# ScalarE writes the upper half of each gelu tile, VectorE only the lower half

## The reference, cut to what matters

```python
h = jax.nn.gelu(jnp.einsum('bsd,edh->bseh', x, w1) + b1, approximate=False)
expert_out = jnp.einsum('bseh,ehd->bsed', h, w2) + b2
out = jnp.einsum('bse,bsed->bsd', gates, expert_out)
```

## Time and profile before

| | |
|---|---|
| median of 3 runs | 2583.78 us (2581.89 to 2583.79) |
| the profiled execution | 2584.22 us |
| its span in the trace | 2582.4 us |
| second half in the trace | from about 1320 us to the end |
| busy over the span | PE 2400.6 us (93%), DVE 1714.1 (66%), ACT 1102.6 (43%), POOL 1118.8 (43%) |
| granted TensorE clock, mean | 0.969 |

### The profile page before, as it was taken

One profiled execution on the slowest core, in us unless ns is written; L12 is line 12 of the kernel. 1 busy time (PEld: TensorE's weight loads), 2 busy tenths in 40 slices (PEclk: granted clock), 3 DMA queues, 4 the chain that ended last, 5 costly groups with the idle time before them and its releaser, 6 DMA issues. The chain is left out here.

```text
span 2582.4 us, 36273 instructions
## 1 busy us (share of the span) xinstructions
PE 2400.6 (93%) x13556; PEld 1007.0 (39%) x13556; DVE 1714.1 (66%) x3957; ACT 1102.6 (43%) x2066; POOL 1118.8 (43%) x404
## 2 busy tenths in 40 slices
PE   7999799999999999999846899999999999999998
PEld 3444223333333232323223454544545454454543
DVE  4433587777777777777125567767676776767665
ACT  4332156666666666666612232323323242332320
POOL 0000369999999999999931112111011211102100
PEclk9999799999999999999968899999999999999999
DMA  7864402122130303130040001010100101010000
GB/s 245 291 226 159 111 11 70 50 52 70 32 91 14 87 25 80 31 104 18 18 156 30 17 1 63 1 53 11 46 17 1 62 1 60 4 46 17 1 17 17
DMA packets 130443, 155.00 MB, mean 60 GB/s; under 512 B 19838, under 2 KB 98174, under 8 KB 129245
## 3 DMA queue, kind: packets, MB, share of 16 engines
q1 hardware_dynamic: 130269, 152.69, 19.2%
HBM read 99.96 MB, written 52.17 MB: 59 GB/s over the span
## 5 line engine op out<-in xcount | busy, mean ns | idle before, releaser
L762 ACT ACTIVATE probs<-st_ps 128x512 f32<-128x512 f32 (+3 forms) x1280 | 610.3, 537 | 327.1 <-PE st_ps L865 179.7
L637 POOL TENSOR_TENSOR total<-total,probs 128x2048 f32<-128x2048 f32 (+3 forms) x200 | 706.5, 3532 | 47.6 <-ACT probs L762 26.6
L804 DVE TENSOR_REDUCE seg_max<-s_ps 128x1 f32<-128x512 f32 x768 | 506.1, 685 | 136.0 <-PE s_ps L851 133.8
L851 PE MATMUL s_ps<-k_pair,q_pair 96*128 96x512 f16 (+3 forms) x1280 | 435.0, 355 | 25.9 <-DMA q_pair<-q_parts 11.4
L865 PE MATMUL st_ps<-q_pair,k_pair 98*128 98x512 f16 (+3 forms) x1280 | 434.4, 353 | 25.7 <-ACT probs L762 16.5
L1429 PE MATMUL fps<-x2T,w_p_hi 128*128 128x512 f16 x1024 | 317.3, 379 | 0.0
L1429 PE MATMUL fps<-w_p_hi,hT 128*128 128x512 f16 x1024 | 306.0, 380 | 0.0
L885 PE MATMUL o_ps<-probs,v_sb 128*32 128x512 f32 (+3 forms) x2560 | 303.0, 546 | 0.0
L808 DVE CUSTOM_DVE_ANT_0 s_ps<-s_ps,later 128x384 f32<-128x384 f32 (+3 forms) x512 | 249.2, 500 | 66.2 <-issue 66.2
L1133 POOL TENSOR_TENSOR rstd<-rstd,keep_power 128x4 f32<-128x4 f32 x24 | 26.1, 1086 | 538.7 <-DVE rstd L1254 538.7
L865 PEld LDWEIGHTS st_ps<-q_pair,k_pair 98*128 98x128 f16 x1280 | 123.3, 98 | 328.1 <-ACT probs L762 233.5
(11 more groups left out here) (164 smaller groups left out, 3401.8 us busy)
## 6 DMA issues: line engine op xcount, KB each, us to landing
k_pair<-k_parts SPq DMA_DIRECT2D x96, 128.0 KB, 4.5
q_pair<-q_parts SPq DMA_DIRECT2D x96, 128.0 KB, 5.1
x_raw<-xT_in SPq DMA_DIRECT2D x8, 1024.0 KB, 6.2
q_parts<-qk_out SPq DMA_DIRECT2D x32, 256.0 KB, 4.1
k_parts<-qk_out SPq DMA_DIRECT2D x32, 256.0 KB, 4.1
piece_raw<-w_in SPq DMA_DIRECT2D x8, 1024.0 KB, 9.1
v_rows<-v_out SPq DMA_DIRECT2D x32, 256.0 KB, 2.1
w_parts<-piece_cut SPq DMA_DIRECT2D x8, 1024.0 KB, 6.0
```

What stands on the lines that cost most here:

```text
L637: last = nc.gpsimd.tensor_tensor(summed[:, :, off:], other[:, :, off:], probs[:, k % NP, :, off:], ALU.add)
L762: nc.scalar.activation(probs[:, k % NP, h, off:], st_ps[:, p % (2 * NVU) % RING, off:], ACT.Exp, scale=SCALE).then_inc(exp_done.sem, 1)
L804: nc.vector.reduce_max(highest, s_ps[:, slot], AX.X).then_inc(s_read.sem, 1)
L851: nc.tensor.matmul(s_ps[:, slot, 0:width], q_pair[a][0:NR, c, h, j * P:(j + 1) * P], k_pair[a][0:NR, h, s * CH:s * CH + width], start=True ...
```

## The change

ACT writes the upper half of each gelu tile itself, right behind the gelu, after waiting for its own gelu to be done. The wait that the upper half's buffer is free (`f_ready`, before the first of an expert's two tiles) moves with it, and the counter `h_hi` is now ACT's. DVE waits for the gelu and for `h_hi`, and writes the lower half as before. In a slot that is 16 instructions that leave DVE's queue and 16 that enter ACT's.

```diff
         @block.scalar
         def _(act):
-            lead(act, (act_read, hi_ready, exped, squared, gate_exped), (gelu_done,))
+            lead(act, (act_read, hi_ready, exped, squared, gate_exped), (gelu_done, h_hi))
...
                     act.wait_ge(h_lo.sem, at(h_lo, i, u, n - 2))
                     nc.scalar.activation(hidden[:, n % 2], fps[:, (u * NUNIT + f) % FB], ACT.Gelu,
                                          bias=W["b1_sb"][:, n:n + 1], scale=UN).then_inc(gelu_done.sem, 1)
+                    act.wait_ge(gelu_done.sem, at(gelu_done, i, u, n))
+                    if j == 0:
+
+                        act.wait_ge(f_ready.sem, at(f_ready, i, u, UNITS.index(("expert", e - 2, TT - 1)) if e >= 2
+                                                    else UNITS.index(("expert", E + e - 2, TT - 1)) - NUNIT))
+                    nc.scalar.activation(hT[:, 0, e % 2, j], hidden[:, n % 2], ACT.Copy,
+                                         scale=XS).then_inc(h_hi.sem, 1)
...
         @block.vector
         def _(dve):
             lead(dve, (dve_read, summed, spread, varied, normed, masked, smaxed, shifted, ssummed, inverted,
-                       square_held, routed), (h_hi, h_lo, added, summed3, spread3, varied3, normed3))
+                       square_held, routed), (h_lo, added, summed3, spread3, varied3, normed3))
...
                 if kind == "hidden":
                     n = 2 * e + j
                     dve.wait_ge(gelu_done.sem, at(gelu_done, i, u, n))
-                    if j == 0:
-
-                        dve.wait_ge(f_ready.sem, at(f_ready, i, u, UNITS.index(("expert", e - 2, TT - 1)) if e >= 2
-                                                    else UNITS.index(("expert", E + e - 2, TT - 1)) - NUNIT))
-                    nc.vector.tensor_scalar(hT[:, 0, e % 2, j], hidden[:, n % 2], XS, None,
-                                            ALU.mult).then_inc(h_hi.sem, 1)
                     dve.wait_ge(h_hi.sem, at(h_hi, i, u, n))
                     nc.vector.scalar_tensor_tensor(hT[:, 1, e % 2, j], hidden[:, n % 2], XS, hT[:, 0, e % 2, j],
                                                    ALU.mult, ALU.subtract).then_inc(h_lo.sem, 1)
```

## The result

| | before | after |
|---|---|---|
| median | 2583.2 us (4 runs) | 2555.22 us (2552.29 to 2556.85, 4 runs) |
| profiled execution, span | 2584.22, 2582.4 us | 2555.81, 2554.0 us |
| granted clock, mean | 0.969 | 0.971 |

The ratio is 0.9891 with a 95% interval of 0.9874 to 0.9908: 28 us, or 1.1%, faster. Forecast was 2554 us.

What follows compares the result with a forecast made beforehand. PE sets the pace, waiting for lower halves of x1T behind a DVE instruction shut out by POOL. Six slots gain 31.4 us, seven lose 1.75, net 29.7: from 2584.22 to 2554.5, so 2554 us; range 2549 to 2570.

Steps and rivals of the forecast that it cites:

- What is shut out, by whom, and what it costs PE: Slots 2 to 7: POOL's addition of bo shuts out DVE's upper half of n 2; PE loses 5.24 us a slot.
- The lower half gets through with 0.12 to 0.38 us to spare: DVE's lower half of n 2 starts that long before POOL's addition of bo, so it is not shut out.
- The upper half on ACT: ACT's copy behind each gelu: 0.05 us wait for its own gelu plus 0.63 us; no added table loads.
- pv1: After the gelu of n 11, ACT's copy delays the probs2 copies; PE waits 0.25 us in seven slots, 1.75 us.
- POOL's later power: POOL's power -0.5, which releases the norm, can end up to 0.26 us later, behind the longer lower half of n 0.
- The sum: Six slots gain 5.24 us each, 31.4 us; seven lose 0.25 each, 1.75 us; net 29.7 us.
- first rival: POOL keeps its precedence: lower half of n 2 shut out in slots 2 to 7; 2583 us, chance 0.10.
- slower rival: ACT is late: upper half over 1.07 us after its gelu, slot 1 gets the wait too; 2593 us, chance 0.05.

Runs made afterwards that it cites:

- n 1 and n 2 alone moved: Kernel before, with only the upper halves of hidden units n 1 and n 2 written by ACT, the other 14 of a slot by DVE: 2553.7 us, ratio 0.9878.
- after, bo added later: Changed kernel, with POOL's addition of bo also waiting until DVE has read the lower halves of x1T: 2552.7 us, ratio 0.9873.
- all but n 2 moved: Kernel before, with 15 of 16 upper halves of a slot on ACT and that of hidden unit n 2 left on DVE: 2584.6 us, ratio 1.0003.
- n 2 alone moved: Kernel before, with only the upper half of hidden unit n 2 on ACT, one of 16 in a slot: 2584.1 us, ratio 1.0004.
- produced at n 2 alone: Changed kernel, with two more ACT copies between the gelu of n 2 and its upper half, about 1.06 us later: 2591.7 us, ratio 1.0026.

## Why the prediction was right, point by point

- *What is shut out, by whom, and what it costs PE.* Shown. With POOL's addition out of the way and DVE untouched, the gain is all there. The loss per slot was put at 5.24 us; the kernels with the wait gone and nothing added have slots of 144.97 against 150.22, 5.25 us.
- *The lower half gets through with 0.12 to 0.38 us to spare.* It was 0.28. POOL's power did come later by the 0.26 us allowed for it: it began 0.15 us behind the lower half of n 0 and took 1.42 us instead of 1.15. But POOL's addition of `bo`, which the prediction let move with the norm or not, did move with it: it began 2.71 us behind the norm's start, where it had begun 2.81 us behind. So only 0.10 of the 0.38 us was lost.
- *The upper half on ACT.* Taken as 0.05 + 0.63 us behind the gelu; it was 0.03 + 0.63. The 29 table loads of the gelu's line stayed 29. The Trainium skill, "ScalarE: Activation LUTs", section "What ACT_TABLE_LOAD costs", gives 0.61 us by its formula (an estimate for 512 elements), close to the 0.63 measured. The same page's advice in "Rules for kernel authors", to use VectorE for a multiplication, decides nothing here: with the multiplication left on VectorE the kernel is 28 us slower than the change in the old order, and as fast as the change once either of POOL's additions is moved.
- *pv1.* Taken as 0.25 us a slot. ACT and PE after, slot 5:

```profile
2111.81 0.63 ACT L1223 ACTIVATE hT<-hidden 128x512 f16<-128x512 f32 x1
2112.35 2.03 ACT L1192 ACTIVATE work<-cps 77x512 f32<-77x512 f32 x4
```

```profile
2112.98 1.06 PE L1484 MATMUL cps<-work,vals 77*32 77x512 f32 x8 [0.17 <-ACT work L1192]
```

  From the scores3 units to the out2 products it is 34.95 us after (2090.92 to 2125.87) and 34.71 with n 1 and n 2 alone moved (2088.32 to 2123.03): 0.24.
- *The term that was missing.* The sum counted POOL's later power against the race, but not against PE, whose transposes wait for the norm. From the out products to the query it is 24.54 us after (2019.31 to 2043.85) and 24.38 with n 1 and n 2 alone moved (2016.88 to 2041.26), where the power is not delayed: 0.16 us in each of slots 2 to 7, 1.0 us. So the slot is 145.38 and not 145.2. Another term that no one forecast worked the other way, by 1.7 us: in the last slot the kernel before ran at the low clock for some 3 us behind its bias products, the profiled execution after did not. The profile of "after, bo added later" hasn't this stretch either, the other eight have it, whether they won the race or lost it; what decides it was not tried. The two rows are before and after.

```profile
2496.50:2498.50 2.00, 2.00 (x7) 0.62 (x5) 0.38 (x1) 0.00 (x0) 0.00 (x0) 0.50 0.03 8
```

```profile
2469.70:2471.70 2.00, 2.00 (x11) 0.88 (x9) 1.42 (x3) 0.00 (x0) 0.00 (x0) 1.00 0.03 8
```

- *The sum.* From the start of slot 1's out products to the end, after is 30.8 us shorter than before, where 29.7 was forecast; ahead of it, after took 2.5 us longer (1435.85 against 1433.39). That forecast and median lie within 1.3 us of each other is in part luck: 1.0 us lost at the norm, 1.7 us won in the last slot and the 2.5 us ahead of slot 1 were in no sum.
- *The price of the rivals.* The first rival was given 0.4 us of gain in each of six slots, since the wait would be that much shorter. With all but n 2 moved, the kernel nearest to it, that gain is there: PE waits 3.10 us instead of 3.58 and the query takes 12.18 us; but pv1 and the norm take it back, and the slot is 150.17. With n 2 alone moved it is not there: the wait was shorter, 3.12 us, but the query took 12.56 us against 12.13, and the slot is 150.19 against 150.22. The slower rival was priced at 9 us, 6.3 of them at pv1. Its mechanism, produced at n 2 alone, cost 7 us beside its own kernel before: the upper half ended 1.70 us behind its gelu there, later than the 1.3 us priced, but pv1 cost no more than after, and slot 1 lost 5.8 us (3.10 of wait and 2.66 in the query) where 5.2 was taken.

## What to carry to other kernels

A mean of 0.72 us that hides a median of 0.43 and a maximum of 4.75 is the line to read first; look for an instruction of POOL that covers the long ones, and ask what waits behind it. Where two engines meet in a race, it is the start times that count: in this kernel moving 15 of 16 instructions gave nothing, moving the right two gave everything, and a wait on POOL's side gave the same without the risk. A gain that rests on 0.28 us is best made safe by an order, since 1 us more on an engine that is idle for half of the time cost all of it and more.

## What the runs showed of the hardware

How close a race can be: DVE 0.08 us behind POOL was shut out for all of POOL's 4.5 us; 0.28 us ahead, in the kernel after, it went through in its usual 0.69 us and POOL took 4.78 us instead of 4.53. No run tried the distances between the two.

A shorter wait of PE need not cost less. In slot 5 of the kernel before, the clock is still granted in full 3 us into PE's wait and comes back at about 2062.8; with only n 2 moved it is at the low level 0.5 us into the wait and comes back at about 2061.8. The rows are the granted clock (eighth column) before, then with n 2 moved, where PE's wait began at 2055.95 and 2054.5.

```profile
2058.00:2059.00 1.00, 0.00 (x0) 0.00 (x0) 1.00 (x3) 0.00 (x0) 0.00 (x0) 1.00 0.00 0
...
2062.50:2063.00 0.50, 0.50 (x3) 0.23 (x2) 0.00 (x0) 0.00 (x0) 0.00 (x0) 0.72 0.00 0
```

```profile
2055.00:2056.00 1.00, 0.00 (x0) 0.00 (x0) 1.00 (x3) 0.00 (x0) 0.00 (x0) 0.50 0.00 0
...
2061.00:2062.00 1.00, 1.00 (x4) 0.40 (x3) 0.00 (x0) 0.00 (x0) 0.00 (x0) 0.62 0.00 0
```

PE's matmuls at the low level are those from 2059.5 to 2062.8 in the one and from 2057.6 to 2061.8 in the other, 3.3 against 4.2 us, which is where the shorter wait's gain went. With all but n 2 moved the wait was as short, 3.10 us, the clock fell only at its end, and the query took 12.18 us. Why the clock fell earlier in the one kernel than in the others was not tried.
